# Pseudo-inverse iteration refactored: the matrix minus identity times the matrix and its companion first, then the polynomial factor times that

## What is computed

```python
s2 = softmax(q_l @ k_l.T)                  # 64 x 64, per head
z = s2.T / (col * row)
for _ in range(6):
    xz = s2 @ z
    z = 0.25 * z @ (13*I - xz @ (15*I - xz @ (7*I - xz)))
out = s1 @ (z @ (s3 @ v))
```

## Time and profile before

| | us |
|---|---|
| median of 3 runs | 1188.13 |
| lowest and highest | 1184.56, 1189.4 |
| the profiled execution | 1187.5 |
| its span, first to last instruction | 1185.5 |
| of it, attention with the six rounds (435 to 802) | 367 |

### The profile page before, as it was taken

One profiled execution on the slowest core, in us unless ns is written; L12 is line 12 of the kernel. 1 busy time (PEld: TensorE's weight loads), 2 busy tenths in 40 slices (PEclk: granted clock), 3 DMA queues, 4 the chain that ended last, 5 costly groups with the idle time before them and its releaser, 6 DMA issues.

```text
span 1185.5 us, 30114 instructions
## 1 busy us (share of the span) xinstructions
PE 1130.5 (95%) x11280; PEld 927.5 (78%) x11281; DVE 764.7 (65%) x1424; ACT 585.5 (49%) x937; POOL 570.4 (48%) x778
## 2 busy tenths in 40 slices
PE   7999999999999688999999999889999999999997
PEld 5888887888887567778778787778888887888885
DVE  6636657676665666867868768555346566676673
ACT  3434246666664445355454453434443255666663
POOL 5720815666675633444433533245402616666664
PEclk9999999999999889999999999999999999999999
DMA  7272143222210300000000000014341232122220
GB/s 248 71 283 109 36 176 115 64 67 70 67 58 25 124 20 2 3 2 3 3 2 2 3 3 3 3 38 159 109 178 36 93 126 71 59 65 64 67 67 14
DMA packets 39456, 80.25 MB, mean 68 GB/s; under 512 B 6436, under 2 KB 31143, under 8 KB 38320
## 3 DMA queue, kind: packets, MB, share of 16 engines
q1 hardware_dynamic: 27824, 53.20, 12.5%
q0 software_dynamic: 11232, 25.20, 6.9%
q10 hardware_dynamic: 288, 0.26, 0.1%
HBM read 57.13 MB, written 27.00 MB: 71 GB/s over the span
## 4 chain that ended last, share of the span: by engine, by line
PE 87%; DVE 7%; ACT 2%; issue 2%; DMA 2%; POOL 1%; ACTq 0%; DVEq 0%; POOLq 0%; SPq 0%
PE PS L1707 18%; PE PS L1621 14%; PE PS L1721 11%; PE PS L1637 7%; PE PS L1911 5%; PE PS L1898 4%; PE PS L1788 4%; PE PS L1714 3%; PE PS L1798 2%; PE PS L1655 2%; DVE A_NM L783 2%; PE PS L1552 2%; PE PS L1858 1%; PE PS L1832 1%; PE PS L1648 1%
## 5 line engine op out<-in xcount | busy, mean ns | idle before, releaser
L1707 PE MATMUL PS<-WHL,XGH 128*128 128x512 f32 x624 | 218.3, 431 | 3.4 <-DVE WHL L662 3.4
L1463 POOL TENSOR_TENSOR A_A<-A_XC,A_ST 128x320 f32<-128x320 f32 (+1 forms) x96 | 73.6, 782 | 178.2 <-ACT A_ST L1187 178.2
L1721 PE MATMUL PS<-WD,XNT 128*128 x624 | 150.5, 384 | 1.5 <-ACT XNT L1121 1.5
L1372 POOL DMA_INDIRECT X<-xs_dram,WHO x78 | 106.2, 1362 | 69.1 <-PE PS L1655 26.2
L683 DVE SCALAR_TENSOR_TENSOR XNT<-PS,SCORES,XNT 128x512 f32<-128x512 f32 x78 | 58.3, 747 | 123.3 <-PE PS L1707 109.3
L1707 PEld LDWEIGHTS PS<-WHL,XGH 128*128 128x128 f32 x624 | 111.8, 190 | 22.4 <-issue 2.8
L1116 ACT ACTIVATE XNT<-PS,SCORES 128x512 f32<-128x512 f32 x78 | 53.7, 688 | 149.0 <-PE PS L1707 148.9
L1721 PEld LDWEIGHTS PS<-WD,XNT 128*128 128x128 f32 x624 | 113.0, 190 | 16.2 <-issue 2.2
L1707 PE MATMUL PS<-WHL,XGL 128*128 128x512 f32 x312 | 123.5, 396 | 0.0
L1637 PE MATMUL PS<-SDH,HHL 128*128 128x256 f32 x512 | 104.8, 288 | 2.1 <-issue 1.5
L1366 POOL TENSOR_SCALAR XNT<-WD 128x128 f32<-128x128 f32 x64 | 49.0, 785 | 118.1 <-DVE WD L556 118.1
(11 more groups left out here) (272 smaller groups left out, 2622.8 us busy)
## 6 DMA issues: line engine op xcount, KB each, us to landing
xs_dram<-WG SPq DMA_DIRECT2D x16, 512.0 KB, 3.0
WU<-in_r_up SPq DMA_DIRECT2D x2, 4096.0 KB, 15.1
shared_dram<-X SPq DMA_DIRECT2D x16, 512.0 KB, 3.1
WG<-in_r_gate SPq DMA_DIRECT2D x2, 4096.0 KB, 18.4
WD<-in_r_down SPq DMA_DIRECT2D x4, 2048.0 KB
X<-in_x SPq DMA_DIRECT2D x8, 512.0 KB, 9.1
X<-mid_dram SPq DMA_DIRECT2D x7, 512.0 KB, 3.8
X<-xs_dram,WHO POOLq DMA_INDIRECT x78
```

The costliest lines, as they stand in the source:

```text
L1372: pool.indirect_dma_start(out=B["XS"][:, u * D:(u + 1) * D], out_offset=None, in_=xs_dram, in_offset=bass.IndirectOffsetOnAxis(ap=B["WHO"] ...
L1463: pool.tensor_tensor(a, x, st, ALU.add).then_inc(att["a"], 1)
L1707: ins = pe.matmul(banks[bank][:], tok, w[:, k * F:(k + 1) * F], start=(k == 0 and i == 0), stop=(k == KD - 1 and i == 2))
L1721: ins = pe.matmul(banks[7][:, 0:D], B["HT"][:, u * F + f * P:u * F + (f + 1) * P], B["WD"][:, bass.ds(ex * (KF * D) + f * D, D)], start=(f ...
```

## The change

The polynomial of a round is factored in another way. With Y scaled by another constant, a round is now

- W = Y - I, on POOL (`chain_w`, new line 1466): two halves of 4 pairs x 64 = 256 columns, read from XC and from the constant `eye2`;
- P = W times [Y|T] on PE (`chain_first`, new line 1902), the weights now from W, the moving side from XC as before;
- ST = 49/11 P + I on DVE (`chain_s`, new line 870), the 64 Y columns of each pair only, 256 columns for a half, in the last round as well; BU = -77/32 P on ACT (`chain_b`), 320 columns, 64 in the last round;
- S times B on PE (`chain_second`, new line 1915), as before;
- XC = 27/32 XC + product on DVE (`chain_x`, new line 881), in place.

`A` and `chain_a` are gone; W has one buffer for all sequences. The products keep their number, their shapes, their order and their partition halves: `landing` returns `HALF[i]` and `IN_QUADRANTS` is `CROSSED`. The factor 3.25 to the sixth in the scale of the result becomes 3.5. A buffer `ROOM` is reserved and not used.

```diff
@@ DVE
-            def chain_b(b, it):
+            def chain_s(b, it):
...
                     if c == 1:
-                        dve.wait_ge(att["st"], count("st", b, 2 * it + 1))
-                    dve.scalar_tensor_tensor(chain_cols(it, c, B["BU"]), chain_cols(it, None, banks[c]), -1.0 / (7 * SCALE[it]),
-                                             chain_cols(it, c, B["XC"][b % 2]), ALU.mult, ALU.add).then_inc(att["bu"], 1)
+                        dve.wait_ge(att["bu"], count("bu", b, 2 * it + 1))
+                    dve.scalar_tensor_tensor(pairs(B["ST"][:])[:, c * PC:(c + 1) * PC, :], pairs(banks[c][:, 0:CW], XW)[:, :, 0:M], Y_ONE,
+                                             const("eye2").unsqueeze(1).broadcast_to([P, PC, M]), ALU.mult, ALU.add).then_inc(att["st"], 1)
@@ DVE
-                for n, c in enumerate((1, 0)):
-                    dve.wait_ge(att["a"], count("a", b, 2 * it + n + 1))
-                    dve.scalar_tensor_tensor(chain_cols(it, c, B["XC"][b % 2]), chain_cols(it, None, banks[c]), -7 / (15 * SCALE[it]),
-                                             chain_cols(it, c, B["A"]), ALU.mult, ALU.add).then_inc(att["x"], 1)
+                for c in (1, 0):
+                    x = chain(b)[:, c * PC:(c + 1) * PC, low:]
+                    dve.scalar_tensor_tensor(x, x, Y_KEPT, pairs(banks[c][:, 0:CW], XW)[:, :, low:], ALU.mult, ALU.add).then_inc(att["x"], 1)
@@ POOL
-            def chain_a(b, it):
+            def chain_w(b, it):
...
                 for n, c in enumerate((1, 0)):
...
+                    if it == 0:
+                        if n == 0:
+                            wait_alone(att["y0"], count("y0", b, 2))
                     else:
-                        a, x, st = (buf[:, part] for buf in (B["A"], B["XC"][b % 2], B["ST"]))
-                    pool.tensor_tensor(a, x, st, ALU.add).then_inc(att["a"], 1)
+                        wait_alone(att["x"], count("x", b, 2 * (it - 1) + n + 1))
+                    part = slice(c * PC, (c + 1) * PC)
+                    pool.tensor_tensor(B["W"][:].rearrange("p (a m) -> p a m", m=M)[:, part, :], B["XC"][b % 2][:].rearrange("p (a w) -> p a w", w=XW)[:, part, 0:M],
+                                       const("eye2").unsqueeze(1).broadcast_to([P, PC, M]), ALU.subtract).then_inc(att["w"], 1)
@@ POOL, the queue
-                chain_a(b, 0)
...
+                chain_w(b, 1)
                 if exists(far):
                     add_bias(far)
-                chain_a(b, 1)
+                chain_w(b, 2)
                 if exists(nxt):
                     s2_normalise(nxt)
-                chain_a(b, 2)
-                chain_a(b, 3)
+                chain_w(b, 3)
...
-                chain_a(b, 4)
+                chain_w(b, 4)
+                chain_w(b, 5)
                 if exists(old):
                     low_outputs(old)
-                chain_a(b, 5)
                 if exists(b):
                     weights_scaled(b)
+                chain_w(nxt, 0)
@@ PE
                 else:
                     pe.wait_ge(att["x"], count("x", b, 2 * it))
+                pe.wait_ge(att["w"], count("w", b, 2 * it + 2))
                 past_waits()
-                for c, p, i in CROSSED:
-                    at = (c * PC + p) * XW
-                    ins = pe.matmul(banks[c][HALF[i], p * XW:(p + 1) * XW], x[HALF[i], at:at + M], x[HALF[i], at:at + XW], start=True, stop=True)
+                for c, p, i in IN_QUADRANTS:
+                    q = c * PC + p
+                    ins = pe.matmul(banks[c][landing(c, i), p * XW:(p + 1) * XW], w[HALF[i], q * M:(q + 1) * M], x[HALF[i], q * XW:(q + 1) * XW], start=True, stop=True)
```

More of the change, by code:

```diff
@@ L290, in count, with landing @@
         return 1 + min(max(b * PER[k] + n, 0), PER[k] * NG)
-    SCALE = [3.25 ** -it for it in range(PINV_ITERS)]
+    Y_SCALE, Y_KEPT, Y_ONE, Y_TWO = 3.5, 27 / 32, 49 / 11, -77 / 32
+    def landing(c, i):
+        return HALF[i]
     V_BANK = (6, 7)
@@ L298, in emit @@
     CROSSED = [(c, p, i) for first in range(2) for p in range(PC) for c, i in ((first, 0), (1 - first, 1))]
+    IN_QUADRANTS = CROSSED
     HALF = [slice(0, M), slice(M, P)]
@@ L829, in column_max @@
                 dve.wait_ge(att["cs"], count("cs", b, 1))
-                dve.tensor_tensor(cs, cs, rs, ALU.mult).then_inc(att["own"], 1)
+                dve.scalar_tensor_tensor(cs, cs, Y_SCALE, rs, ALU.mult, ALU.mult).then_inc(att["own"], 1)
                 dve.wait_ge(att["own"], count("own", b, 3))
@@ L919, in attention_vector @@
                 done, old, nxt, far, ln = b - 2, b - 1, b + 1, b + 2, b + 3
-                chain_b(b, 0)
+                chain_s(b, 0)
                 if b == NG - 1:
@@ L936, in attention_vector @@
                     s3_max(nxt, 1)
-                chain_b(b, 1)
+                chain_s(b, 1)
                 if exists(far):
@@ L946, in attention_vector @@
                     s2_sum(nxt)
-                chain_b(b, 2)
+                chain_s(b, 2)
                 if exists(ln):
@@ L957, in attention_vector @@
                     landmarks(far, 0, 0)
-                chain_b(b, 3)
+                chain_s(b, 3)
                 if exists(done):
@@ L966, in attention_vector @@
                     row_max(nxt)
-                chain_b(b, 4)
+                chain_s(b, 4)
                 if exists(old):
@@ L976, in attention_vector @@
                     s1_max(nxt, 1, (0,))
-                chain_b(b, 5)
+                chain_s(b, 5)
                 if b == NG - 1:
@@ L1177, in values, with chain_b @@
                          banks[V_BANK[jj]][:].rearrange("p (n d) -> p n d", d=HS)).then_inc(att["v_sb"], 1)
-            def chain_s(b, it):
+            def chain_b(b, it):
                 if not exists(b):
                     return
+                low = M if it == PINV_ITERS - 1 else 0
                 act.wait_ge(att["c1_ready"], count("c1_ready", b, it + 1))
@@ L1185, in chain_s @@
                     if c == 0:
-                        act.wait_ge(att["bu"], count("bu", b, 2 * it + 1))
-                    act.mul(B["ST"][:, c * CW:(c + 1) * CW], banks[c][:, 0:CW], -15 / (13 * SCALE[it])).then_inc(att["st"], 1)
+                        act.wait_ge(att["st"], count("st", b, 2 * it + 1))
+                    bu, product = (x.rearrange("p (a w) -> p a w", w=XW)[:, :, low:] for x in (B["BU"][:, c * CW:(c + 1) * CW], banks[c][:, 0:CW]))
+                    act.mul(bu, product, Y_TWO).then_inc(att["bu"], 1)
             def numerators(b, c):
@@ L1230, in attention_scalar @@
                     numerators(old, 0)
-                chain_s(b, 0)
+                chain_b(b, 0)
                 if exists(old):
@@ L1241, in attention_scalar @@
                     turned(far, 1)
-                chain_s(b, 1)
+                chain_b(b, 1)
                 if exists(nxt):
@@ L1247, in attention_scalar @@
                         values(nxt, 0)
-                chain_s(b, 2)
+                chain_b(b, 2)
                 if exists(nxt):
@@ L1260, in attention_scalar @@
                     exp1(b, 0)
-                chain_s(b, 3)
+                chain_b(b, 3)
                 if exists(nxt):
@@ L1270, in attention_scalar @@
                     projected(far, 1)
-                chain_s(b, 4)
+                chain_b(b, 4)
                 if exists(far):
@@ L1281, in attention_scalar @@
                     first_deviation_of_batches()
-                chain_s(b, 5)
+                chain_b(b, 5)
                 if exists(far):
@@ L1908, in chain_second @@
                 past_waits()
-                for c, p, i in CROSSED:
-                    at = (c * PC + p) * XW
-                    ins = pe.matmul(banks[c][HALF[i], p * XW + low:(p + 1) * XW], B["ST"][HALF[i], at:at + M], B["BU"][HALF[i], at + low:at + XW],
+                for c, p, i in IN_QUADRANTS:
+                    q = c * PC + p
+                    ins = pe.matmul(banks[c][landing(c, i), p * XW + low:(p + 1) * XW], B["ST"][HALF[i], q * M:(q + 1) * M], B["BU"][HALF[i], q * XW + low:(q + 1) * XW],
                                     start=True, stop=True)
```

17 lines of the change are left out of this document (5 added, 12 removed).

## The result

| | before | after |
|---|---|---|
| median of 4 runs each, us | 1188.74 | 1209.03 |
| lowest and highest | 1184.56, 1189.4 | 1204.76, 1212.58 |
| the profiled execution | 1187.5 | 1212.04 |
| its span | 1185.5 | 1210.2 |

The ratio is 1.017, with a 95% interval of 1.015 to 1.019. The changed kernel is 20.3 us slower, and the forecast was 1210. The profiled execution is near the slow end of its four, 24.5 us above that of before; what can be said of the few us between them stands at the experiment with idle products.

The account below looks back on a forecast made before the run. PE, busy 95% of the span, was taken to bound the kernel. PE's waits for W (19.6 us) plus `low_outputs` meeting DVE (3) gave 22.6 on 1187.5, so 1210 us, range 1196 to 1219.

Parts of the forecast that it names:

- W's length and the distance: POOL's W takes 0.725 us a half; start of XC's update to PE's next first product becomes 2.22 us (2.01 to 2.49).
- The 0.15 by which KLS might hold up W: Round two: the small DVE step after XC's update may delay W's second half, raising the wait from 0.89 to 1.0 us.
- An ordinary period: Sequences 1 to 5: waits for W in rounds two, three and six, four and five covered; 2.2 us each, 11.0 together.
- The port term: `low_outputs`, moved behind the sixth W on POOL, holds up DVE's `column_max`: 0 to 1.0 us in six periods, 3 taken.
- the bound's: Skill's shared port rule, for any step size with two SBUF inputs on DVE: `low_outputs` costs 6 us, total 1213.7.
- The start of the next sequence: First round's W behind the halves of `start_y`: 2.48 us needed, 2.47 there, so cost 0.
- Sequences 0, 6 and 7: Waits for W in the other periods: 1.65 us without round two, 2.6 with thinner filler, 4.4 with the chain bare.
- the signs that the prediction named: Trace after: W 0.72 a half, distances 2.2, PE waiting 12 to 20 us, busy time unchanged, period 50.3, `column_max` over 0.5.
- Rival 2: W takes 0.86 us a half and `low_outputs` hinders DVE every time: 32 us more, 1219; chance 0.15.
- Rival 4: The period's slack takes all of W: no change, within 0.5% (5.9 us); chance 0.08.
- Rival 3: PE absorbs most: W at 0.62 us, no port cost, DVE sets the pace; +7 us, 1195; chance 0.17.
- Rival 5: Shorter ACT and DVE halves and no A shorten the way between products, W costing nothing: 1181 us; chance 0.05.

Follow-up runs that it names:

- the experiment with idle products: Changed kernel plus six idle 128-column products on PE ahead of the wait for W, rounds two to five of sequence 7 only: 1208.23 us, ratio 1.0162.
- the side effects away: Changed kernel with `low_outputs` at the end of POOL's period, period 5's root ahead of the fifth W, and idle products in sequence 7: 1202.98 us, ratio 1.0122.
- the run beside them: The changed kernel itself, unedited, run a second time as control: 1211.51 us, ratio 1.0187.
- the last experiment: Changed kernel with W of rounds two to six on DVE, `low_outputs` late, period 5's root moved, idle products in sequence 7: 1202.35 us, ratio 1.0113.

## Why the prediction was right, step by step

**W's length and the distance.** Predicted 0.725 a half and 2.22; measured 0.71 (1.42 for two, which overlap a little; a single record is 0.73) and 2.16 to 2.20. Interpolating between A's two sizes was good to 3%. The 0.15 by which KLS might hold up W did not come: KLS was held up instead (0.69 for 0.21).

**An ordinary period.** Predicted 0.8 + 0.7 + 0 + 0 + 0.67 = 2.2 us. Measured from first product to first product in sequences 2, 4 and 5: 0.84 to 0.86, 0.43 to 0.45, 0, 0, 0.55 to 0.57, together 1.85. The 0.8 is what the prediction had left at round two's second product, behind 1.0 at its first, so the first two measured steps are to be laid beside its 1.5 us. What was swallowed there is the term that was mis-sized. The prediction had 0.2 of the first wait swallowed at the second product, and 0.25 more at XC's update (from 0.8 to 0.55). The second product of sequence 3 stands 11.04 us behind the sequence's start, before it was 10.52: 0.52 late, so 0.33 of 0.85 were swallowed. The update is 12.52 against 12.15: 0.37 late. Then W adds 2.18 - 1.26 = 0.92, and the sum, 1.29, is what the two rounds show. Rounds four and five were free, as read from their 2.76 and more. The prediction's remark that sequences 1 to 5 agree to some hundredths overlooked that sequence 1 has 1.74 ahead of round three and 3.74 ahead of round five.

**The port term.** Predicted 0 to 1.0 us a period, the half taken. The mechanism is the bound's. After the change:

```profile
576.76 2.54 POOL L1488 TENSOR_TENSOR A_OTL<-A_OT,A_OTH 128x512 fp32r<-128x512 f32 x2
...
577.09 0.98 DVE L839 SCALAR_TENSOR_TENSOR A_MR<-A_SM,CB 128x16 f32<-128x16 f32 x1
```

DVE's step, 0.17 before, ends when POOL's running half ends (576.76 + 1.27 = 578.03; 577.09 + 0.98 = 578.07), and in sequence 6 `column_max` on 8 columns takes 1.20. L835 two steps ahead, on 8 columns, took 0.24 instead of 0.17 and ended where W's second half did (576.82 and 576.80); L837, with one input, took 0.20 as before, although `low_outputs` was running. The rule of the Trainium skill, SBUF — State Buffer, section "SBUF: two separate sides", by which the two engines hold a port pair for a whole instruction, was so borne out on steps of 8 and 16 columns too. But the price on the path was not 0.8 to 1.0 a period. It was 0.2 to 0.3, as the move of `low_outputs` showed, while without the wait for W the same move brought 0.7 to 0.8. A likely reading: 0.57 of it fall into the time that round six is late anyway. That was worked out, not isolated. So of the predicted 3 us, 6 x 0.27 = 1.6 came, if period 6 paid like the others.

**The start of the next sequence.** Predicted 0, because 2.48 was needed and 2.47 there: the distance is 2.45 in six of the seven periods with filler, 2.63 in sequence 3.

**Sequences 0, 6 and 7.** Predicted 1.65, 2.6 and 4.4; the profile has 2.3, 7.6 and 6.5. With the clock left at its full level in sequence 7, and the side effects away, they are 1.2, 3.2 and 4.7, the last with about 1 us that the idle products themselves add in two rounds (distance 2.72 instead of 2.17). So the readings of the narrow places were near, and what the profile has above them is mostly the granted clock. The prediction has no term for it. It is worth 2.4 us in sequence 7 and 3.3 in the whole by the run with idle products, and 3.3 to 4.9 us in periods 6 and 7 came also where nobody waited for W.

**The total.** Predicted 22.6 us: 19.6 for the wait, 3 for the port. Measured 20.3: about 14.3 for the wait, and 6 for port, clock and the interplay of the two. The total was within 2.3 us because the wait was some 5 us smaller than its term and the missing clock term made up for it. The mechanism and the direction were right; that the total came so near was in part luck. Part of the 5 us lies in the trace of before: it had a stretch at the lower clock in sequence 1 and a wide round six in sequence 3 (2.08), so that these two periods grew by 0.5 and 1.6 only. Of the signs that the prediction named, the distances, W's length and the step of over 0.5 us in `column_max` came; PE's waits for W were 22.5 us instead of 12 to 20, its busy time did not stay, and the ordinary period was 49.5 to 49.7 instead of 50.3.

**The rivals.** Rival 2 (W dearer) falls with W's 0.71 a half, though its other part, `low_outputs` in DVE's way every time, came true; it cost less than was thought. Rival 4 (no change) falls with the ratio. Rival 3 (PE absorbs most) had its mechanism in round three, 0.34 and more swallowed, but not its size. Rival 5 (faster) had the bound: with W costing nothing the rest gives 1186.3, not 1181.

## What to carry to other kernels

A step between two products costs its duration, less the slack of that place, at each round, whatever its engine's busy share; read the slack as the distance from the last producer to the consumer, round by round, and add the new step's length and hop to it. When an engine comes onto the path, all else in its queue comes with it: a 4 us job ahead of the step, and every instruction of it that a DVE step with two SBUF inputs can meet. And where filler is thin, look at the granted clock behind an added wait: it can be paid twice, once as idle time and once in PE's clock. One profile of each kernel is not enough to say so, since the low stretches come in kernels without that wait too.

## What was not expected of the hardware

- Waits of PE of 1.0 to 2.2 us were in many places followed by 2 to 8 us at a granted clock of 0.50, in which a step of 32 products took up to 2.40 instead of 1.32 us, and in others (446 us before the change) were not. Most dips stood nearly at the same places when the same kernel was run again (446, 770, 780 to 788, 794 to 798 and 804 to 808 us; one was at 740 instead of 750); they moved with each edit. That the kernel's own runs differ, 1204.8 to 1212.6, at mean clocks of 0.985 and 0.978, points to the same cause, though only the one profile was read for that.
- `KLS`, a DVE step with a single SBUF input and 128 columns, took 0.21 us in six of seven sequences before, 0.69 beside W on POOL (first timeline above), 0.21 where W was on DVE. XC's update with one SBUF and one PSUM input kept 0.87 to 0.89 beside a running POOL step (539.70 in the last experiment). So one input from SBUF does not by itself spare a DVE step from meeting POOL, though L837 above was spared.
- Six idle products of 128 columns, 1.6 us of PE time ahead of a wait of 2.2, were no dearer than leaving PE idle, and by the run beside them 3.3 us cheaper; two of the four rounds then had a distance of 2.72 instead of 2.17.
